# One more dense unit of the first half before the second half's sorted tiles, two units instead of three after them

## The reference

```
x = x + tanh(g_xattn[0]) * attention_16_heads(layernorm(x), ctx)
x = x + tanh(g_ffn[0])   * top2_of_8_experts_relu(layernorm(x))      # hidden 256
x = x + tanh(g_xattn[1]) * attention_1_head(layernorm(x), ctx)
x = x + tanh(g_ffn[1])   * second_block(layernorm(x))                # hidden 512

# second_block, for xf of 1024 x 128
logits = relu(xf @ Wr1 + br1) @ Wr2 + br2
gates  = softmax(logits); tg, ti = top_k(gates, 2); tg = softmax(tg / 2)
out = silu(xf @ Ws1 + bs1) @ Ws2 + bs2                               # the shared expert
for e in range(8):
    h = silu(xf @ We1[e] + be1[e]) @ We2[e] + be2[e]
    out = out + sum(tg * (ti == e)) * h                              # zero weight for tokens not sent to e
```

## Time and profile before

| what | value |
|---|---|
| median of three runs | 320.46 us |
| profiled execution | 320.1 us, span 318.3 us |
| TensorE matmul busy | 283.4 us, 89% of the span |
| VectorE busy | 191.1 us, 60% |
| ScalarE busy | 164.7 us, 52% |
| POOL busy | 88.5 us, 28% |
| mean granted TensorE clock | 0.974 of full |

### The profile page before, as it was taken

How to read it: one execution, slowest core, us unless ns; L and a number is a source line. 1 busy time by engine, 2 the same in 40 slices (tenths; PEclk the granted TensorE clock), 3 DMA queues, 4 the chain that set the end, 5 groups by cost and what they waited for, 6 DMA issues and landing times.

```text
span 318.3 us, 6215 instructions
## 1 busy us (share of the span) xinstructions
PE 283.4 (89%) x2157; PEld 243.6 (77%) x2157; DVE 191.1 (60%) x595; ACT 164.7 (52%) x352; POOL 88.5 (28%) x132
## 2 busy tenths in 40 slices
PE   1999986989989988899998999989989948999993
PEld 0577854878868776798977997869778948999892
DVE  3789845688899976337768486557748421222024
ACT  3483456778876666313353735865147304564630
POOL 1265012578854332011037410101005310000341
PEclk9999999799999999989999999999999986999998
DMA  7699810000000000440000000000001847211112
GB/s 194 226 320 241 224 42 2 1 4 5 26 2 2 3 0 2 150 152 0 0 2 0 2 1 3 0 0 2 1 0 35 268 134 217 69 35 34 43 33 83
DMA packets 21006, 20.37 MB, mean 64 GB/s; under 512 B 1921, under 2 KB 15641, under 8 KB 20976
## 3 DMA queue, kind: packets, MB, share of 16 engines
q1 hardware_dynamic: 20080, 18.57, 19.7%
q0 software_dynamic: 896, 1.41, 2.0%
HBM read 15.84 MB, written 4.13 MB: 63 GB/s over the span
## 4 chain that ended last, share of the span: by engine, by line
PE 51%; DVE 20%; DMA 10%; POOL 8%; issue 7%; ACT 3%; SPq 1%; POOLq 0%; DVEq 0%; ACTq 0%
PE bank L1406 9%; PE bank L1387 5%; PE bank L1200 5%; DVE xhat_sb L896 4%; PE bank L1202 4%; PE bank L1394 4%; PE bank L1201 4%; DMA xs_hbm<-xhat_sb,slots_sb 4%; PE bank L1185 3%; POOL p_sb L630 3%; DVE sum_sb L833 3%; DMA w_q_sb<-ys_hbm,y_slots_sb 3%; PE bank L1227 2%; PE bank L1145 2%; DMA ctx_tok_sb<-in_ctx 2%
## 5 line engine op out<-in xcount | busy, mean ns | idle before, releaser
L770 ACT ACTIVATE hT_sb<-bank,cols_sb 128x512 f32<-128x512 f32 x72 | 48.7, 689 | 59.7 <-PE bank L1202 59.3
L630 POOL TENSOR_TENSOR p_sb<-p_sb,recip_sb 128x480 f32<-128x480 f32 x32 | 31.6, 987 | 52.2 <-DVE recip_sb L836 52.2
L1122 DVE SCALAR_TENSOR_TENSOR x_sb<-bank,wts_sb,x_sb 128x128 f32<-128x128 f32 x96 | 27.0, 344 | 29.2 <-PE bank L1406 19.0
L1227 PEld LDWEIGHTS bank<-we_sb,hT_sb 128*128 128x128 f32 x320 | 37.0, 192 | 1.1 <-issue 0.5
L1227 PE MATMUL bank<-we_sb,hT_sb 128*128 128x128 f32 x320 | 37.7, 275 | 0.0
L1406 PEld LDWEIGHTS bank<-w_sb,hT_sb 128*128 128x128 f32 x256 | 32.1, 200 | 1.2 <-issue 0.4
L1406 PE MATMUL bank<-w_sb,hT_sb 128*128 128x128 f32 x256 | 33.0, 285 | 0.0
L780 ACT ACTIVATE p_sb<-bank,bias_t_sb 128x128 f32<-128x128 f32 x60 | 17.2, 368 | 25.3 <-PE bank L1387 25.3
L679 POOL TENSOR_TENSOR rstd_sb<-veps_sb,minus_half_sb 128x4 f32<-128x4 f32 (+1 forms) x11 | 10.6, 959 | 70.6 <-DVE veps_sb L888 70.3
L1156 PE MATMUL bank<-ident_sb,p_sb 128*120 128x128 f32 x128 | 20.0, 282 | 7.7 <-POOL p_sb L630 7.4
L1156 PEld LDWEIGHTS bank<-ident_sb,p_sb 128*120 128x120 f32 x128 | 13.6, 138 | 11.6 <-issue 10.1
(11 more groups left out here) (213 smaller groups left out, 609.6 us busy)
## 6 DMA issues: line engine op xcount, KB each, us to landing
xs_hbm<-col_rows_sb SPq DMA_DIRECT2D x1, 2048.0 KB, 14.0
we_sb<-in_L_ffn_We SPq DMA_DIRECT2D x1, 2048.0 KB, 9.1
w_sb<-in_L_ffn_We SPq DMA_DIRECT2D x8, 256.0 KB, 4.7
w_after_sb<-in_L_ffn_We SPq DMA_DIRECT2D x7, 256.0 KB, 2.8
w_kv_sb<-in_L_xattn_w_kv SPq DMA_DIRECT2D x2, 512.0 KB, 6.7
w_sb<-in_L_ffn_w SPq DMA_DIRECT2D x1, 1024.0 KB, 10.3
w_kv_sb<-xs_hbm SPq DMA_DIRECT2D x15, 64.0 KB, 2.1
ys_hbm<-w_kv_sb SPq DMA_DIRECT2D x3, 256.0 KB, 2.3
```

The costliest lines, as they stand in the source:

```text
L630: nc.gpsimd.tensor_tensor(p0[j % 4], p0[j % 4], recip0[:, j % 2, :].unsqueeze(2) .broadcast_to([128, HG, SK]), ALU.mult).then_inc(probs_re ...
L770: nc.scalar.activation(hT[:, u % 2, c, :], ps(item)[:, :], ACT.Relu if n == 1 else ACT.Silu, bias=cols[:, col:col + 1]).then_inc(read(item ...
L1122: last = nc.vector.scalar_tensor_tensor(out=x[:, b, :], in0=ps(item)[:, C * i:C * (i + 1)], scalar=w, in1=x[:, b, :], op0=ALU.mult, op1=AL ...
L1227: last = nc.tensor.matmul(ps(key)[:, C * i:C * (i + 1)], hT[:, unit_at[(n, p, e)] % 2, c, 128 * i:128 * (i + 1)], we2[:, e, c, :], start=( ...
```

## The change

One number: `AHEAD`, the count of half 0's routed experts that are worked on ahead of the tiles, goes from 6 to 7. Unit `(3, 0, 6)` moves from behind the tiles to ahead of them. No operation is added or removed.

```diff
-    AHEAD = 6
+    AHEAD = 7
     ahead_of_tiles = [(3, 0, E)] + [(3, 0, e) for e in range(AHEAD)]
     behind_tiles = [(3, 1, E)] + [(3, 0, e) for e in range(AHEAD, E)]
     units = expert_units(0) + expert_units(1) + ahead_of_tiles + behind_tiles
```

## The result

The changed kernel took **322.31 us** (median of ten runs, 320.82 to 323.10), the kernel before 319.92 us in ten runs beside it (319.01 to 321.25). The ratio is 1.0072, with a 95% interval of 1.0051 to 1.0093: 0.7% slower, 2.4 us. The forecast was 322.6 us. The changed kernel's profiled execution took 322.25 us and has a span of 320.5 us, 2.2 us more than before.

The account below looks back on a forecast made before the run. The prediction took the gathers, which hang on the last tile, to end last. From the profiled 320.1 us, +2.88 (later first product) - 2.08 (old slow start gone) + 1.71 (new clock spell) = 322.6 us, range 320.0 to 324.3.

Parts of the forecast that it names:

- first product later: Start of the tiles: TensorE's first tile product begins at 266.60 us, 2.88 us later than before.
- first to third product above full clock: First tiles on TensorE: one spell at half clock adds 1.71 us to the products.
- end of the last tile later: End of the tiles: the last tile and all that hangs on it come 2.51 us later.
- TensorE ahead of the last gather's landing: Program end: TensorE finishes its units at 308.98 us, the last gather pair lands at 316.21, 7 us later.
- The new wait: Ahead of the first tile: VectorE does its 1.13 us `down` before copying the transposes; TensorE idles 2.2 us.
- The clock: First tiles: one half-clock spell of 3.4 us, +1.71 us, chosen between bounds of 0 and 3.4 us; chance 0.50.
- The rival by which the clock holds: First tiles: the clock stays full over the new idle time, giving 320.9 us; chance 0.32.
- the place that I went by, at 54 us: Earlier TensorE place, idle 1.70 and 0.71 us around four transposes; the clock fell for 3.42 us, costing products 1.71 us.
- A unit ahead is paid in full, and taking one from behind gives nothing back: Around the tiles: the unit's parts ahead end 6.43 us later; 6.43 us taken off TensorE behind are worth nothing.
- The rival of two spells: First tiles: the clock stays down for two spells, 3.4 us in place of 1.71, 324.3 us; chance 0.10.
- The collision of stores and gathers: Program end: three 64 KB stores between the gathers slow three pairs, adding 3.1 us, 325.7 us; chance 0.06.
- the rival *Faster: Program end: TensorE sets the end; smaller form, first gather pair quick, gives 1.0 us, 321.6 us; chance 0.02 over 1%.

Follow-up runs that it names:

- e2: Changed kernel with only VectorE's order altered: the copy of the first transposes before the last unit's `down`; 320.56 us, ratio 1.0017.
- e3: Changed kernel with 16 unread identity transposes added on TensorE in the idle place before the first tile; 320.27 us, ratio 1.0015.
- e4: Kernel before with unread identity transposes on TensorE, 30 before the first real ones and 11 before the first tile; 317.05 us, ratio 0.9915.
- e1: Changed kernel with the first four tiles' transposes and their copy one unit's parts earlier; 320.01 us, ratio 1.0003.
- e6: Kernel before with five routed experts ahead of the tiles (`AHEAD` 5) and four units behind; 324.38 us, ratio 1.0145.
- e7: Changed kernel with two gather pairs in flight on POOL instead of one; 318.07 us, ratio 0.9941.
- e5: Changed kernel with one more unit, `(3, 1, E)`, ahead of the tiles and only `(3, 0, 7)` behind; 327.36 us, ratio 1.0236.
- e8: Kernel before with two gather pairs in flight on POOL instead of one; 318.87 us, ratio 0.9968.
- e10: Changed kernel with the first transposes in the middle of the last unit's parts and two gather pairs in flight; 313.95 us, ratio 0.9821.
- e11: e10 with six routed experts ahead and two pairs of POOL's scatters in flight too; 315.51 us, ratio 0.9907.
- e9: Changed kernel with the first transposes in the middle of the last unit's parts; 318.77 us, ratio 0.9981.

## Why the prediction was right

The time was forecast at 322.6 us and measured at 322.31. By its steps, each from the mark so that the 0.73 us don't count (the mark is at 238.07 before and at 237.34 after):

| step | forecast | measured |
|---|---|---|
| first product later | 2.88 | 28.44 - 25.65 = 2.79 |
| TensorE idle ahead of it | 2.2 | 2.18 |
| slow spell | 3.4 | 3.4 |
| first to third product above full clock | 1.71 | 4.09 - 2.22 = 1.87 |
| end of the last tile later | 2.51 | 58.32 - 55.74 = 2.58 |
| TensorE ahead of the last gather's landing | 7.2 | 315.85 - 308.40 = 7.45 |

- **The new wait** is right to 0.1 us, and its cause, the `down` ahead of the copy, is shown by e2: without it 0.73 us of the 2.18 are gone. The sum's 2.88 us for the later first product are also seen in e3 against e4, 3.2 us.
- **The clock** was the step that I had to choose between bounds, and the choice came out right: one spell of 3.4 us. e3 prices it at 1.8 us, and e4 prices the longer one of the kernel before at 2.7. The rival by which the clock holds would have given 320.9 us, and e3, where it is made to hold, gives 320.3. But the place that I went by, at 54 us, was weak evidence, and that it pointed the right way was in part luck: among the thirteen traces of this document a spell began there in nine, and in four (changed kernel, e1, e6, e7) the clock held over the same idle times. The Trainium skill's rule (TensorE: Matmul & The Clock Gate, section Why this matters for your kernels) of gaps over about 3 us, taken as a safe limit, does not agree with these traces: 2.18 us sufficed in the three profiled executions that had that gap, the changed kernel, e5 and e7.
- **A unit ahead is paid in full, and taking one from behind gives nothing back** as long as the gathers end last: e5 shows it. e6 shows the limit, as with four units behind TensorE ends last and the fourth one costs time. That the gathers set the changed kernel's end is shown by e7.
- **The rival of two spells** did not come about. **The collision of stores and gathers** did not either: with three stores between them the four pairs took 15.99 us, less than the 16.72 before, and just at the edge of the 16 to 18 us that the prediction had named. The smaller form of the rival *Faster* did come: the first pair took 303.86 - 299.86 = 4.00 us instead of 4.95, as quick as the others.
- **What the sum left out** are two terms of opposite sign: the last store of results took 3.06 us instead of 2.04, and the gathers 0.73 us less. With the 0.73 us from the mark they come to -0.4 us; the span's own difference, 2.2 us, is 2.58 + 1.02 - 0.73 - 0.73 = 2.14 us, and 0.06 us at the very end. That both would cancel was luck.

## What to carry to other kernels

Idle time of an engine is not a reason by itself to move work into it: ask whether what is moved stands ahead of the chain that ends the program or beside it. Where work is put ahead of a chain, look at every engine's queue at the seam; here a 1.1 us addition that nobody needed yet stood ahead of the one copy on the path, and the gap that it helped to make cost another 1.9 us by the clock. When two ends meet within a microsecond, relieving one of them alone is worth little (e8: 1.0 us, where the same edit gives 4.2 in e7).

## What the runs showed of the hardware

- The clock's fall can come after the idle time, and then hits the work behind it. After 2.18 us of idle time the clock was still full when the products began and went to half 0.3 us into them, for 3.4 us (in e7 0.1 us, in e5 0.6 us into them). After 1.45 us (e2) and 1.56 us (the wait for routing, in all thirteen traces) it did not fall.
- The length of the gap doesn't settle it. At two places ahead of the mark the work is the same in every kernel here, and yet at 54 to 57 us (idle 1.70 us, then at most 0.71) a spell began in nine traces of thirteen, and behind the idle times of 0.27 and 0.93 us at 130 to 133 us also in nine, not in e4, e8, e10 and e11. Such spells come and go between executions of equal work. The 2.18 us have three traces to stand on, all with a spell.
- Forty-one transposes of an identity on TensorE, in time that was idle anyway, made a kernel 0.85% faster (e4).
- The last store of results shows two kinds of times in otherwise equal kernels: 2.0 us (kernel before, e5, e6, e8, e11) or 2.6 to 3.7 us (changed kernel, e1 to e4, e7, e9, e10). It is 1 us on the chain at the end, as large as several of the terms above. What decides it was not found.
- POOL's indirect transfers do not need to wait for each other in pairs: with two pairs in flight POOL issues one every 1.25 to 1.4 us (e7) instead of two per 4.0 us. In e8 VectorE and ScalarE each started one instruction 2.3 and 3.0 us late meanwhile.
